# Softplus's parts added by TensorE, dt in x's tile, stages placed by a table of times

## The reference

```python
xh, z = split(ln(x) @ W_in)                   # 512 + 512 channels
xc = depthwise_conv3x3(xh)
dt_r, B, C = split(xc @ W_xproj)              # 8, 16, 16
dt = softplus(dt_r @ W_dt + b_dt)             # 512 a position
dtN = dt @ W_dtN + b_dtN                      # 16 a position
# scan over the 2304 positions of an image, 8 images at once
h = exp(-dt * exp(A_log)) * h + (dtN * B) * xc     # 512 x 16 states
y = h @ C + Dskip * xc
x = x + (ln(y) * ln_g + ln_b) * silu(z) @ W_out + b_out
t = ln(x); a = ln(x) > 0.5                    # FFN: nibbles of channels 32.., 40.., 48..
x = x + t + shifted_nibbles(a)                # added to channels 64 to 87
```

## Time and profile before

| | |
|---|---|
| median of 3 runs | 4027.85 us (4012.58 to 4034.44) |
| profiled execution | 4022.24 us, span 4020.4 us |
| mean granted clock of TensorE | 0.854 of full |
| DVE busy | 3622.2 us, 90% |
| PE busy | 3251.8 us, 81% |
| POOL busy | 3133.2 us, 78% |
| ACT busy | 2944.1 us, 73% |
| DMA | 790.26 MB, mean 197 GB/s |

### The profile page before, as it was taken

One profiled execution on the slowest core, in us unless ns is written; L12 is line 12 of the kernel. 1 busy time (PEld: TensorE's weight loads), 2 busy tenths in 40 slices (PEclk: granted clock), 3 DMA queues, 4 the chain that ended last, 5 costly groups with the idle time before them and its releaser, 6 DMA issues.

```text
span 4020.4 us, 103342 instructions
## 1 busy us (share of the span) xinstructions
PE 3251.8 (81%) x33792; PEld 1589.3 (40%) x33792; DVE 3622.2 (90%) x12317; ACT 2944.1 (73%) x6050; POOL 3133.2 (78%) x5771
## 2 busy tenths in 40 slices
PE   5788888888888888888888888888888888888665
PEld 2334433443344334433443344344433343444333
DVE  2799999999999999999999999999999999999996
ACT  3677777777777787777777777777777777787663
POOL 0788877888888788877888788778877888788874
PEclk7889887889889988988898889888888798889776
DMA  3877878788878787878787878787877888788773
GB/s 67 219 202 203 213 191 206 190 208 205 208 196 214 199 211 196 215 194 205 197 216 199 207 196 213 199 205 193 206 201 199 201 203 209 202 206 205 192 192 80
DMA packets 383392, 790.26 MB, mean 197 GB/s; under 512 B 80517, under 2 KB 235142, under 8 KB 382854
## 3 DMA queue, kind: packets, MB, share of 16 engines
q1 hardware_dynamic: 382854, 783.66, 77.1%
HBM read 648.18 MB, written 96.73 MB: 185 GB/s over the span
## 4 chain that ended last, share of the span: by engine, by line
DVE 31%; PE 31%; ACT 26%; issue 7%; SPq 3%; POOL 2%; DMA 1%; ACTq 0%; POOLq 0%; DVEq 0%
ACT ps_a L638 8%; PE ps_s L583 6%; DVE h L885 6%; PE ps_y L492 6%; PE ps_s L528 4%; DVE ps_a L869 4%; DVE ps_a L872 4%; DVE h L888 4%; PE ps_s L537 3%; ACT ap L648 3%; PE ps_s L566 3%; PE ps_y L476 2%; ACT y L721 2%; DVE sz L941 2%; PE ps_s L584 2%
## 5 line engine op out<-in xcount | busy, mean ns | idle before, releaser
L638 ACT ACTIVATE ps_a<-dtb,a_n 128x384 f32<-128x384 f32 x2304 | 1253.6, 583 | 488.1 <-DVE h L888 472.3
L1169 POOL TENSOR_TENSOR h<-mp,up 128x128 f32<-128x128 f32 x2304 | 1052.5, 457 | 357.6 <-PE ps_y L492 147.4
L1159 POOL TENSOR_TENSOR mp<-ap,h 128x128 f32<-128x128 f32 x2304 | 1051.9, 457 | 358.1 <-ACT ap L648 242.7
L869 DVE TENSOR_TENSOR ps_a<-ps_a,h 128x192 f32<-128x192 f32 x2304 | 813.6, 353 | 239.6 <-ACT ps_a L638 236.7
L885 DVE SCALAR_TENSOR_TENSOR h<-xb,db,ps_a 128x192 f32<-128x192 f32 x2304 | 921.9, 400 | 24.0 <-PE ps_y L492 16.0
L888 DVE SCALAR_TENSOR_TENSOR h<-xb,db,ps_a 128x192 f32<-128x192 f32 x2304 | 927.2, 402 | 0.0
L492 PE MATMUL ps_y<-h,cw 64*32 64x256 f32 x18432 | 787.9, 461 | 71.9 <-DVE h L888 58.0
L872 DVE TENSOR_TENSOR ps_a<-ps_a,h 128x192 f32<-128x192 f32 x2304 | 807.7, 351 | 0.0
L648 ACT ACTIVATE ap<-dtb,a_n 128x256 f32<-128x256 f32 x1152 | 524.2, 509 | 251.1 <-DMA dtb<-xd 233.9
L1149 POOL TENSOR_TENSOR up<-xb,db 128x512 f32<-128x512 f32 x576 | 610.8, 1060 | 3.0 <-DMA xb<-xd 3.0
L492 PEld LDWEIGHTS ps_y<-h,cw 64*32 64x32 f32 x18432 | 315.7, 122 | 488.2 <-DVE h L888 244.6
(11 more groups left out here) (111 smaller groups left out, 4286.5 us busy)
## 6 DMA issues: line engine op xcount, KB each, us to landing
xb<-xd SPq DMA_DIRECT2D x576, 512.0 KB, 7.2
dtb<-xd SPq DMA_DIRECT2D x576, 512.0 KB, 6.3
xs<-xh SPq DMA_DIRECT2D x196, 192.0 KB, 6.2
xd<-dttok SPq DMA_DIRECT2D x288, 128.0 KB, 5.4
xin<-in_x_dram SPq DMA_DIRECT2D x144, 128.0 KB, 6.2
xd<-xtok SPq DMA_DIRECT2D x192, 96.0 KB
res<-in_x_dram SPq DMA_DIRECT2D x144, 128.0 KB, 5.4
out_dram<-res SPq DMA_DIRECT2D x144, 128.0 KB, 3.9
```

What stands on the lines that cost most here:

```text
L638: ins = act.activation(ps_a[buf][:, n, 0:2 * VD].rearrange("p (t d) -> p t d", t=2), dtb[:, u % DUNITS, 2 * buf:2 * buf + 2, 0:VD], ACT.Ex ...
L869: dve.tensor_tensor(a[:, 0], a[:, 0], last[:, 0], ALU.mult).then_inc(m0_done, 1)
L1159: pool.tensor_tensor(mp[:, G % 2], ap[:, Q % 2, G % 4], h[:, (G - 1) % HRING, :, VD:HALF], ALU.mult) \
L1169: pool.tensor_tensor(h[:, G % HRING, :, VD:HALF], mp[:, G % 2], up[:, Q % 2, G % 4], ALU.add) \
```

## The change

The SLOT and AHEAD tables give way to one table AT: for each stage the steps at which its parts are issued, counted from step 0 of the row's own scan (so -47 is step 1 of the row before, and 98 is step 2 of the second row after). It now also holds the steps on ACT, DVE, POOL and SP. ACT copies run one step after PE's part (COPY_LAG), the stores of x and dt two steps after, each block on its own. Compared with before, `dttok` is at steps 22, 24, 25 instead of 23, 24, 26, `dtn` at 26 instead of 27, `out` at 29, 30, 32 instead of 29, 30, 31, POOL's gate four times at 22 instead of 21 to 24, `stack` at 22 instead of 8, `store` at 12 instead of 6, `bounce` at 25 instead of 30, `states` at 42 instead of 34, the reload of ACT's table at 45 instead of 38, and the FFN at 2 to 12 of the second row after instead of 40 to 48 of the first; the loops run one row further.

The relu part has a tile of its own, `rel`. `finish_dt` is gone: `transpose_dt` multiplies both parts with the identity and adds them in PSUM, and `dtn_project` multiplies both with W_dtN. dt by tokens is copied into `xtok`, after x's stores have landed. `x_project`, `dt_project` and `dtn_project` work on two halves of 192 tokens in the lower and the upper 64 partitions; weights for `wdt` and the bias are loaded twice. The FFN compares with 0.5 inside the instructions that use it, masks the nibble with 15 in place of `found`, and handles both nibbles' marks in one instruction.

```diff
-B_ROW, C_ROW, XP_ROWS = 32, 64, 80
+
+B_ROW, C_ROW, XP_ROWS = 32, 48, 64
...
+HTOK, HSIDE = TOK // 2, SIDE // 2
...
-SLOT = {
-    "conv": (0, 1, 3, 4), "xproj": (6,), "dtp": (8, 9, 11, 12), "xtok": (14, 15, 16), "yt": (18, 19, 20, 21),
-    "dttok": (23, 24, 26), "dtn": (27,), "out": (29, 30, 31), "z": (33, 34, 36, 37), "xlnT": (39, 40),
-    "proj": (42, 43, 45, 46),
+
+AT = {
+    "conv": (-47, -46, -45, -44), "xproj": (-43,), "dtp": (-42, -42, -39, -39), "xtok": (-35, -34, -33),
+    "dttok": (-26, -24, -23), "dtn": (-22,), "yt": (64, 65, 66, 67), "out": (77, 78, 80), "z": (33, 34, 36, 37),
+    "xlnT": (-154, -153), "proj": (-149, -148, -146, -144), "exp": (-39, -33), "log": (-35, -31),
+    "copy_y": (21, 36, 51), "y_log": (56,), "y_scale": (57,), "y_norm": (58, 58, 61), "ln1_log": (-172,),
+    "ln1_scale": (-171,), "reload": (45,), "ln2_log": (95,), "ln2_scale": (95,), "ln1_apply": (-164, -162, -162),
+    "y_stats": (21, 45, 52), "y_shift": (57,), "residual": (78, 80, 82), "ln2_stats": (80, 83, 83),
+    "sz": (35, 36, 36, 37), "make_db": (-20,), "ln1_stats": (-183, -183, -177), "ln1_shift": (-164,),
+    "ffn": (98, 98, 99, 99, 100, 100, 101, 101, 102, 105, 106, 106, 107, 107, 108, 108), "cw": (-4, 7, 26),
+    "gate": (70, 70, 70, 70), "store": (108,), "stack": (-122,), "load_res": (66,), "bounce": (-23,), "states": (-6,),
+    "load_xin": (-197,),
 }
-
-AHEAD = {"conv": 1, "xproj": 1, "xtok": 1, "dtp": 1, "dttok": 1, "dtn": 1, "xlnT": 4, "proj": 4, "z": 0, "yt": -1, "out": -1}
-FIRST_ROW, LAST_ROW = -4, SIDE
+SHARED = ("conv", "xproj", "dtp", "xtok", "dttok", "dtn", "yt", "out", "z", "xlnT", "proj")
+FIRST_ROW, LAST_ROW = -4, SIDE + 1
+COPY_LAG, STORE_LAG = 1, 2
...
+def due(stage, i, s, lag=0):
+
+    places = [(i - (at + lag) // SIDE, j) for j, at in enumerate(AT[stage]) if (at + lag) % SIDE == s]
+    return [(r, j) for r, j in places if exists(r)]
...
-        xp = sb("xp", [XP_ROWS, IMAGES, SIDE])
-        dbt = sb("dbt", [B_ROW + NS, IMAGES, SIDE])
+        xp = sb("xp", [P, IMAGES, HSIDE])
+        dbt = sb("dbt", [P, IMAGES, HSIDE])
         dt = sb("dt", [P, NG, TOK])
         xtok = sb("xtok", [P, KT, DI])
-        dttok = sb("dttok", [P, KT * DI])
+        rel = sb("rel", [P, NG, TOK])
...
-            def store_dt(r):
-                sp.wait_ge(dttok_ready, r * KT + KT)
-                if r >= 2:
+            def store_dt(r, k):
+                sp.wait_ge(dttok_ready, r * KT + k + 1)
+                if r >= 2 and k == 0:
                     for n in range(DUNITS):
                         sp.wait_ge(dt_loaded[n], (r - 1) * (QUADS // DUNITS) * SEM_DMA)
-                for k in range(KT):
-                    for half in range(2):
-                        sp.dma_start(xd[r % 2, 1, half, :, 16 * k:16 * k + 16, :].rearrange("b w d -> w b d"),
-                                     dttok[:, k * DI + half * HALF:k * DI + (half + 1) * HALF]) \
-                          .then_inc(dt_stored, SEM_DMA)
+                for half in range(2):
+                    sp.dma_start(xd[r % 2, 1, half, :, 16 * k:16 * k + 16, :].rearrange("b w d -> w b d"),
+                                 xtok[:, k, half * HALF:(half + 1) * HALF]) \
+                      .then_inc(dt_stored, SEM_DMA)
...
-                for which, src in ((0, dbt[B_ROW:B_ROW + NS]), (1, xp[C_ROW:C_ROW + NS])):
-                    sp.dma_start(bounce[r % 2, which].rearrange("b n w -> n b w"), src).then_inc(bounced, SEM_DMA)
+                for which, src, row in ((0, dbt, B_ROW), (1, xp, C_ROW)):
+                    for half in range(2):
+                        lo = half * XP_ROWS + row
+                        sp.dma_start(bounce[r % 2, which, :, :, half * HSIDE:(half + 1) * HSIDE].rearrange("b n w -> n b w"),
+                                     src[lo:lo + NS]).then_inc(bounced, SEM_DMA)
...
+                    for r, j in due("store", i, s):
+                        store(r)
+                    for r, j in due("stack", i, s):
+                        load_stack(r)
+                    if i + 1 - AT["stack"][0] // SIDE == SIDE + 1 and s == AT["stack"][0] % SIDE:
+                        load_stack(SIDE)
+                    for r, j in due("load_res", i, s):
+                        load_residual(r)
+                    for r, j in due("xtok", i, s, STORE_LAG):
+                        store_x(r, j)
+                    for r, j in due("dttok", i, s, STORE_LAG):
+                        store_dt(r, j)
+                    for r, j in due("bounce", i, s):
+                        bounce_states(r)
+                    for r, j in due("states", i, s):
+                        load_states(r)
...
-                    mm = pe.matmul(bank[0:XP_ROWS, 0:TOK], wxp[:, g, :], by_step(xc[:, r % 2, g, :]),
-                                   start=g == 0, stop=g == NG - 1)
+                    for half in range(2):
+                        lo = half * XP_ROWS
+                        mm = pe.matmul(bank[lo:lo + XP_ROWS, 0:HTOK], wxp[:, g, :],
+                                       by_step(xc[:, r % 2, g, :])[:, half * QUADS // 2:(half + 1) * QUADS // 2],
+                                       start=g == 0, stop=g == NG - 1, skip_group_check=True)
...
+                banks = [take_bank("dtp", r, 2 * pair + half) for half in range(2)]
+                for n in range(2):
+                    g = 2 * pair + n
+                    for half in range(2):
+                        rows = slice(half * XP_ROWS, half * XP_ROWS + DTR + 1)
+                        mm = pe.matmul(banks[half][:, n * HTOK:(n + 1) * HTOK], wdt[rows, g * P:(g + 1) * P],
+                                       xp[rows].rearrange("p b w -> p w b"), start=n == 0, stop=n == 1,
+                                       skip_group_check=True)
...
-                    pe.wait_ge(dt_ready, r * 2 + 2)
+                    pe.wait_ge(sp_log, r * 2 + 2)
                 bank = take_bank("dttok", r, k)
                 for g in range(NG):
-                    mm = pe.transpose(bank[:, g * P:(g + 1) * P], dt[:, g, k * P:(k + 1) * P], ident[:])
+                    pe.matmul(bank[:, g * P:(g + 1) * P], rel[:, g, k * P:(k + 1) * P], ident[:], start=g == 0, stop=False,
+                              skip_group_check=True)
+                    mm = pe.matmul(bank[:, g * P:(g + 1) * P], dt[:, g, k * P:(k + 1) * P], ident[:], start=False,
+                                   stop=g == NG - 1, skip_group_check=True)
                 mm.then_inc(dttok_done, 1)
 
             def dtn_project(r):
-                pe.wait_ge(dt_ready, r * 2 + 2)
+                pe.wait_ge(sp_log, r * 2 + 2)
                 bank = take_bank("dtn", r, 0)
                 for g in range(NG):
-                    mm = pe.matmul(bank[0:B_ROW + NS, 0:TOK], wdtn[:, g, :], dt[:, g, :],
-                                   start=g == 0, stop=g == NG - 1)
+                    for part in (rel, dt):
+                        for half in range(2):
+                            lo = half * XP_ROWS
+                            mm = pe.matmul(bank[lo:lo + XP_ROWS, 0:HTOK], wdtn[:, g, :],
+                                           part[:, g, half * HTOK:(half + 1) * HTOK], start=g == 0 and part is rel,
+                                           stop=g == NG - 1 and part is dt, skip_group_check=True)
...
             def copy_xtok(r, k):
                 act.wait_ge(xtok_done, r * KT + k + 1)
                 if r >= 1 and k == 0:
-                    act.wait_ge(x_stored, r * 2 * len(X_PARTS) * SEM_DMA)
+                    act.wait_ge(dt_stored, r * 2 * KT * SEM_DMA)
                 act.activation(xtok[:, k, :], shared_bank("xtok", r, k)[:], ACT.Copy).then_inc(xtok_ready, 1)
 
             def copy_dttok(r, k):
                 act.wait_ge(dttok_done, r * KT + k + 1)
-                act.activation(dttok[:, k * DI:(k + 1) * DI], shared_bank("dttok", r, k)[:], ACT.Copy) \
+                if k == 0:
+                    act.wait_ge(x_stored, (r + 1) * 2 * len(X_PARTS) * SEM_DMA)
+                act.activation(xtok[:, k, :], shared_bank("dttok", r, k)[:], ACT.Copy) \
                    .then_inc(dttok_ready, 1)
 
             def softplus_parts(r, g):
 
                 act.wait_ge(dtp_done, r * NG + g + 1)
                 if r >= 1 and g == 0:
-                    act.wait_ge(dt_stored, r * 2 * KT * SEM_DMA)
+                    act.wait_ge(dttok_done, r * KT)
                     act.wait_ge(dtn_done, r)
-                bank = shared_bank("dtp", r, g)[:, 0:TOK]
-                act.activation(dt[:, g, :], bank, ACT.Abs).then_inc(sp_abs, 1)
-                act.activation(dttok[:, g * TOK:(g + 1) * TOK], bank, ACT.Relu).then_inc(sp_relu, 1)
+                bank = shared_bank("dtp", r, g)[:, 0:TOK].rearrange("p (n t) -> p n t", n=2)
+                groups, half = slice(g // 2 * 2, g // 2 * 2 + 2), slice(g % 2 * HTOK, (g % 2 + 1) * HTOK)
+                act.activation(dt[:, groups, half], bank, ACT.Abs).then_inc(sp_abs, 1)
```

(32 more changed lines are left out.)

376 lines of the change are left out of this document (165 added, 211 removed).

## The result

The changed kernel takes 4073.11 us (median of 4 runs, 4049.18 to 4076.56), the kernel before in the same sessions 4024.05. The ratio is 1.011, 95% interval 1.006 to 1.016: about 1% slower, where 4% faster was forecast. The profiled execution has a span of 4070.8 us, 50.4 more than before.

What follows compares the result with a forecast made beforehand. DVE's own work plus the places where it stands bound the kernel; 1.8 us less work and 1.8 less idle a row save 173 us over 48 rows, +5 for start and end: 4022 to 3855 us, range 3710 to 4000.

Steps and rivals of the forecast that it cites:

- part 5: Placement of DMAs and FFN: earlier dtb ends most of a 1.8 us stall; idle 4.0 us a row instead of 5.8.
- Rival (b): Shared tile: x stores land 2 us later, DVE stands 4.1 us a row, 3950 us; chance 0.16.
- Part 1: DVE instructions removed or merged: 1.8 us a row saved, between 0.0 and 2.3.
- Rival (e): DVE's waits pass to the next instructions: only 0.7 us a row saved instead of 1.8, 3908 us; chance 0.10.
- Part 3: TensorE's new dt matmuls and halved projections: +1.8 us a row of TensorE work, harmless on average.
- the tie: Between state sums at steps 24 and 28, TensorE needs 10.2 us against DVE's 10.0: 0.2 us.
- (c): TensorE cancels the gain: halves do not overlap, dt blocks cost 0.2 us an instruction; about 4030 us, chance 0.12.
- (d): TensorE's clock stays at 1.2 GHz through steps 22 to 28: 6.2 us a row of standing, 4150 us; chance 0.10.
- Part 4: ACT's first dt copy, step 23, waits for x stores in the shared tile; DVE stands 2.1 us at step 24.
- The FFN's move: FFN stages go from steps 40 to 47 to steps 2 to 12; DVE's missing 3.9 us shrink to about 1.
- Start and end: Outside the scan: six more weight loads and row 46's FFN after the scan, +5 us.

Runs made afterwards that it cites:

- small and big DMAs: Changed kernel with stack at step 8, plus at step 22 four unused DMAs of 256 bytes (small: 3911.5 us) or 192 KB (big: 4078.3 us).
- e4_old_places: Changed kernel with the whole table AT set to the steps of the kernel before: 4111.7 us, 1.0247 of the kernel before.
- the own tile: Changed kernel with dt by tokens in its own tile: 4062.3 us; with stack at step 8 too, 3917.2; with bounce at step 29 as well, 3858.6.
- the two numbers changed: Changed kernel with stack at step 8 instead of 22 and bounce at step 29 instead of 25: 3858.2 us, 0.9585 of the kernel before.

## Why the prediction was wrong

**The step that failed is in part 5**: "so `dtb` of step 24 goes out 12.3 us after step 16; now it is 2085.59, about 14.3 us after [...]: DVE's stall at step 32, most of the 1.8 us that it misses in 2076 to 2094, goes." It did not go; in the mean over rows it grew from 1.6 to 3.4 us. Two terms were off. The issue time was mis-sized: with step 16 at 1461.3 the load goes out at 1477.13, 15.8 us after, because SP comes late into that stretch (`xb` of step 16 is 1.8 us late behind the first group of x stores) and three residual loads take 2.87 us instead of 2.0. That is 4.3 us after DVE is ready for step 24 (1472.80), no better than before, where it was 4.45 (2085.59 against 2081.14). (The 14.3 us of before were a slip as well: L869 of step 16 starts at 2069.01, so steps 16 to 19 took 6.8 us and not 4.7; DVE stood in them.) Worse, I gave `stack` only its issues and left the landing time at the 6.3 us that the trace of before showed for a load with no 768 KB ahead of it. It became 10.5 us. The small and big DMAs show that the second term is the one that costs: a moved DMA has to be charged for its bytes in front of whatever is behind it, and I had charged only its issues. I had put DVE's idle at 4.0 us a row. In the mean over rows it was 8.9, with the stack early 5.3, and with the bounce later too 4.3. Rival (b) came nearest in kind (full DMA queues), but put the cost at the x stores, and taking that wait away gained nothing.

**Part 1, right, at its upper end.** DVE's work fell by 2.3 us a row, where I took 1.8 between 0.0 and 2.3. Rival (e), in which the waits pass on and 0.7 us is left, fell as a sum. Single lines did move, in both directions:

```profile
L1007 DVE TENSOR_SCALAR res<-res,sc 128x256 f32<-128x256 f32 x144 | 89.3, 672 | 0.1
...
L947 DVE SCALAR_TENSOR_TENSOR dbt<-ps_s,bdtn,xp 128x192 f32<-128x192 f32 x48 | 19.6, 408 | 40.6 <-PE ps_s L601 40.6
...
L1021 DVE TENSOR_SCALAR nib<-nib 128x9 int32<-128x9 int32 x48 | 13.8, 287 | 0.0
```

L1007, which was L976 before, took 500 ns then and 672 at its new steps; `make_db` came out at 0.41 us, as worked out; the AND in place of L992 at 0.29. The Trainium skill (SBUF — State Buffer, Who interferes with whom) says that DVE in a 2-port mode and GpSimd block each other for a whole instruction. That L1007 got longer at other steps fits this, but no run here tells how much of a line's mean is the lock.

**Part 3, too dear in size, and the tie came back by another way.** The new matmuls, from TensorE's timeline at steps 25 and 26:

```profile
1473.16 0.39 PE L588 MATMUL ps_s<-ident,rel 128*128 128x128 f32 x2
1473.38 0.39 PE L590 MATMUL ps_s<-ident,dt 128*128 128x128 f32 x2
...
1476.31 0.49 PE L601 MATMUL ps_s<-dt,wdtn 128*64 128x192 f32 x4
1476.63 0.49 PE L601 MATMUL ps_s<-rel,wdtn 128*64 128x192 f32 x4
```

Two instructions in 0.22 us, 0.111 each, a little under my lower bound of 0.116 (I took 0.165): 5.3 us a row, not 7.9. The 0.165 was a misreading of the earlier trace rows: 0.66 us is four transposes with the end of the last one's pipeline, and inside they start 0.11 us apart too (2080.04, 2080.15, 2080.26). Four halves of `dtn_project` in 0.32 us, eight groups in 2.6: they overlap fully, as taken. The tie at step 28 did not bind where I had put it: DVE's L916 waits 11.9 us in all for the sum of the states. But TensorE has no time left in that stretch, and once the wait for the x stores is taken away, ACT's copies wait for the same dt blocks (120.0 and 101.5 us), and DVE for ACT at steps 26 and 28. Rivals (c) and (d) fell in the changed kernel as I had priced them: the halves of `dtn_project` overlap, and the granted clock is 0.95 in steps 20 to 31. e4_old_places shows that it takes the new places to keep TensorE's work harmless; which of them, no run tells.

**Part 4, right and without effect.** I had the wait at 2.1 us a row of DVE; ACT waits 99.0 / 47 = 2.1 us and DVE stands about 1.4 at step 24. Yet the own tile gains nothing, since ACT then waits for TensorE's dt blocks. I had added it to the sum as a loss of its own; taken away alone it is worth nothing.

**Part 5, the rest.** The FFN's move did what I said at steps 9 to 19 (idle 3.9 to 1.0), and is worth far more than I gave it. The bounce I costed "at nothing, and at the 1 us of a late ACT if that cover is gone": it was nothing with the stack late, 0.018 x 4023 / 48 = 1.5 us with it early. Start and end came to +7.6 and -3.6 us against +5 for both. With the two numbers changed the kernel runs at 3858 us, beside my 3855; that the sums meet is partly chance, since the terms differ (2.3 for 1.8 of work; idle 4.6 for 4.0, of which step 24 has 1.3 and not 2.1).

## What to carry to other kernels

When a stage moves, charge its DMAs twice: for the issues on their queue, and for their bytes ahead of each load that is behind them and has a due time; the landing time read from the trace before holds only for the traffic that was ahead of the load then. No fixed price per byte comes out of these runs (0.9 us and 4.2 us for the same 768 KB), so a run that moves this one stage back, and one that puts its bytes there and nothing else, are worth their time. A wait that is late but covered gains nothing when it is removed, and may gain much once what covers it is gone (the bounce: 0 and then 1.8%), so test such edits again after each repair. When removing a wait changes nothing, read the waits again before calling it harmless: here one edit moved the wait from the stores to TensorE, and another traded late dt for a late residual. Work saved on the busiest engine pays only where that engine is what ends the stretch.

## What the runs showed of the hardware

The same 512 KB load, behind other traffic, was used 6.3, 7.2, 7.7, 10.5 and 12.9 us after its issue: before; before with `stack` at step 22 (e9_before_late_stack); behind four DMAs of 256 bytes; in the changed kernel behind the four of `stack`; and behind four of 192 KB from DRAM to DRAM. ACT was waiting for it each time. Four issues on SP take 2.5 us for 256 bytes each as for 192 KB each; the four of `stack`, also 192 KB each, took 2.8 to 3.3.

A float32 matmul instruction with 128 columns against a 128 x 128 stationary side starts 0.111 us after the one before it at full granted clock, and a float32 transpose of the same size 0.109 us, the same within the resolution. The halves of `dtn_project`, 64 columns of the array each, overlap fully: four instructions of 192 columns in 0.32 us from start to start, as long as one of 384 took before. The halves of `dt_project`, nine rows each at partitions 0 and 64, take 2.10 us for eight instructions of 192 columns, 0.26 each, against 0.69 for one of 384 before: halving the columns and running two row halves side by side gave a factor of 1.3 for the whole, not the 2 that I took.
